# Layer norm of the router inputs in a macaron block: one tile of four on ScalarE, statistics and normalizations interleaved on VectorE

## What is computed

```python
def _layernorm(x, axis=-1, eps=1e-05):
    m = jnp.mean(x, axis=axis, keepdims=True)
    v = jnp.var(x, axis=axis, keepdims=True)
    return (x - m) / jnp.sqrt(v + eps)

x = x + 0.5 * _L0_ffn_ref(_layernorm(x, axis=-1), router_w, wg, wu, wd)
x = x + _L0_attn_ref(_layernorm(x, axis=-1), Wq, bq, Wk, bk, Wv, bv, Wo, bo)
x = x + 0.5 * _L0_ffn_ref(_layernorm(x, axis=-1), router_w, wg, wu, wd)

# in _L0_ffn_ref: router, top two of eight, and the experts
logits = xf @ router_w.T
probs = jax.nn.softmax(logits, axis=-1)
topw, topi = jax.lax.top_k(probs, K)
...
eo = jnp.einsum('ecf,efd->ecd', jax.nn.silu(g) * u, wd)
```

## Time and profile before

| | us |
|---|---|
| median of 3 runs | 1919.36 (1918.79 to 1923.34) |
| profiled execution, its own time | 1917.76 |
| span in the profile | 1916.0 |
| busy PE, PEld | 1616.2, 1275.8 |
| busy DVE, ACT, POOL | 1246.2, 887.6, 874.8 |

### The profile page before, as it was taken

How to read it: one execution, slowest core, us unless ns; L and a number is a source line. 1 busy time by engine, 2 the same in 40 slices (tenths; PEclk the granted TensorE clock), 3 DMA queues, 4 the chain that set the end, 5 groups by cost and what they waited for, 6 DMA issues and landing times.

```text
span 1916.0 us, 40317 instructions
## 1 busy us (share of the span) xinstructions
PE 1616.2 (84%) x13943; PEld 1275.8 (67%) x13943; DVE 1246.2 (65%) x2883; ACT 887.6 (46%) x1627; POOL 874.8 (46%) x636
## 2 busy tenths in 40 slices
PE   4512899999999999995899751289999999999998
PEld 3411687877878787773577641168787787878876
DVE  8987748576574856526898897763745546465551
ACT  4511445445454444535665551144544545445452
POOL 5623262644536354235776652326264452635423
PEclk9999999999999999996999755589999999999999
DMA  6650461614425152226766450045161442515212
GB/s 214 212 185 14 108 122 30 145 41 107 78 70 126 37 132 52 31 29 165 154 146 146 137 195 4 14 108 116 36 145 44 104 83 65 128 42 126 58 25 28
DMA packets 261236, 182.16 MB, mean 95 GB/s; under 512 B 160938, under 2 KB 247860, under 8 KB 261172
## 3 DMA queue, kind: packets, MB, share of 16 engines
q1 hardware_dynamic: 230452, 139.37, 26.7%
q0 software_dynamic: 30720, 41.96, 13.2%
HBM read 89.01 MB, written 54.53 MB: 75 GB/s over the span
## 4 chain that ended last, share of the span: by engine, by line
PE 72%; DVE 12%; issue 6%; POOL 5%; DMA 2%; ACT 2%; DVEq 0%; SPq 0%; POOLq 0%; ACTq 0%
PE bank L1439 43%; PE bank L1452 22%; PE bank L1420 3%; POOL rstd L418 1%; POOL rows L422 1%; DVE kT L1020 1%; DVE rT L1020 1%; PE bank L1400 1%; DVE gat L1229 1%; PE bank L1484 1%; ACT xn L778 1%; DMA xs<-in_L_attn_x 1%; POOL gat L395 1%; DVE xn L937 1%; DVE v L1223 1%
## 5 line engine op out<-in xcount | busy, mean ns | idle before, releaser
L1439 PE MATMUL bank<-xT,w_g 128*128 128x320 f16 x3072 | 503.1, 300 | 30.9 <-DMA xT<-gat 30.9
L1095 DVE SCALAR_TENSOR_TENSOR unit_buf<-bank,sc_cur,unit_buf 128x320 f32<-128x320 f32 x512 | 281.5, 550 | 353.9 <-PE bank L1439 227.9
L1439 PE MATMUL bank<-xT,w_u 128*128 128x320 f16 x3072 | 502.5, 300 | 0.0
L720 ACT ACTIVATE unit_buf<-bank,sc_cur 128x320 f32<-128x320 f32 x512 | 269.5, 526 | 407.1 <-PE bank L1439 405.6
L1452 PE MATMUL bank<-w_d,xs 128*128 128x256 f16 x3840 | 423.8, 273 | 0.0
L1452 PEld LDWEIGHTS bank<-w_d,xs 128*128 128x128 f16 x3840 | 375.2, 98 | 44.4
L1439 PEld LDWEIGHTS bank<-xT,w_g 128*128 128x128 f16 x3072 | 295.7, 99 | 141.0 <-issue 30.6
L389 POOL TENSOR_TENSOR hot_v<-hot_b,val 128x400 bf16<-128x400 bf16 x128 | 147.7, 1154 | 519.9 <-DVE hot_b L1078 519.9
L1439 PEld LDWEIGHTS bank<-xT,w_u 128*128 128x128 f16 x3072 | 301.3, 98 | 117.7
L1101 DVE TENSOR_TENSOR xs<-unit_buf,xs 128x320 f16<-128x320 f32 x512 | 268.0, 523 | 2.2
L395 POOL DMA_INDIRECT gat<-rows_d,id_next x160 | 177.0, 1106 | 200.4 <-DVE id_next L1088 140.0
(11 more groups left out here) (229 smaller groups left out, 1815.2 us busy)
## 6 DMA issues: line engine op xcount, KB each, us to landing
rows_d<-rows SPq DMA_DIRECT2D x32, 512.0 KB, 3.4
raw_gu<-in_L_ffn_wg SPq DMA_DIRECT2D x16, 1024.0 KB, 6.3
raw_gu<-in_L_ffn_wu SPq DMA_DIRECT2D x16, 1024.0 KB, 9.3
raw_d<-in_L_ffn_wd SPq DMA_DIRECT2D x16, 1024.0 KB, 5.5
x_d<-xs SPq DMA_DIRECT2D x1, 8192.0 KB, 32.6
out_x<-xs SPq DMA_DIRECT2D x16, 512.0 KB, 3.7
xs<-in_L_attn_x SPq DMA_DIRECT2D x7, 1024.0 KB, 5.6
xs<-x_d SPq DMA_DIRECT2D x5, 1024.0 KB, 6.1
```

Source lines behind the costliest of these rows:

```text
L720: act.activation(act_s[:, u % 2, :], bank[u % 2][:, 0:CW], ACT.Silu, scale=sc_cur[:, 3:4]).then_inc(S.s_ready, 1)
L1095: dve.scalar_tensor_tensor(h32[:, u % HB, :], bank[2 + u % 2][:, 0:CW], sc_cur[:, 4:5], act_s[:, u % 2, :], mult, mult).then_inc(S.h32_rea ...
L1439: mm = pe.matmul(bank[2 * m + u % 2][:, 0:CW], wgu[m][:, w, k, f * P:(f + 1) * P], xT[:, a * KD + k, c * CW:(c + 1) * CW], start=(j == 0 a ...
```

## The change

ScalarE normalizes the last tile of each group of four (`ACT_TILE`, L671 of the changed kernel), as x times `rstd` plus `nmean`, where `nmean` is minus the mean times `rstd`: VectorE takes minus the mean out of `mv` (one new operation), GpSimd multiplies it with `rstd` behind `power` (one new operation). A semaphore `s_xact` counts ScalarE's tiles; ScalarE waits for it before `high`, and VectorE waits for it before it overwrites `nmean`. VectorE has three `norm` left in a group. A new function `turn(i, r)` issues them between the parts of the next group's statistics: four `bn_stats`, `norm` 0, four `bn_aggr`, `norm` 1, `nmean` and the variance, `norm` 2. The calls of `beside` come two at a time behind each `turn`; before, one stood behind each `stats` and each `norm`. In the second stage ScalarE also waits for `at.lo` before its first tile.

```diff
--- before.py
+++ after.py
@@ -190,6 +190,7 @@
         s_bootx = sem("boot_scale_steps")
         s_passed = sem("waits_passed")
         s_atw = sem("attention_loaded")
+        s_xact = sem("norm_by_act_ready")
 
         def ffn_sems(p):
             names = ("loaded kept stat_ready rstd_ready xn_ready hi_ready lo_ready stored0 stored1 turned turned_ok cent_ready "
@@ -336,6 +337,7 @@
             b, j = q
             return 16 * (QUADS // 2 * b + j // 2 + 1)
 
+        ACT_TILE = G4 - 1
         xt2_flat = xt2[:, :, :, :, :].rearrange("p h t c n -> p h (t c n)")
         FIRST = STEPS - 2
         TURN_BANK = (0, 3)
@@ -416,6 +418,8 @@
                 def power(q, r):
                     pool.wait_ge(S.stat_ready, q + 1)
                     pool.tensor_tensor(rstd[:, r, :], rstd[:, r, :], mhalf[:, :], ALU.pow).then_inc(S.rstd_ready, 1)
+                    pool.wait_ge(S.rstd_ready, 2 * q + 1)
+                    pool.tensor_tensor(nmean[:, r, 0:1], nmean[:, r, 0:1], rstd[:, r, ACT_TILE:], mult).then_inc(S.rstd_ready, 1)
 
                 def low(q, r):
                     pool.wait_ge(S.hi_ready, q + 1)
@@ -662,6 +666,11 @@
 
             def ffn_in(S, head, beside):
                 def high(i, r):
+                    act.wait_ge(S.rstd_ready, 4 * i + 2 * r + 2)
+                    act.wait_ge(S.lo_ready, 2 * i + r + 1)
+                    act.activation(xn[:, r, ACT_TILE, :], tiles(xs, i * PAIR + r * G4 + ACT_TILE, 1)[:, 0], ACT.Identity,
+                                   scale=rstd[:, r, ACT_TILE:], bias=nmean[:, r, 0:1]).then_inc(s_xact, 1)
+                    act.wait_ge(s_xact, 2 * i + r + 1 + (2 * STEPS if S.scaled else 0))
                     act.wait_ge((S.stored0, S.stored1)[r], 16 * i + 16)
                     act.wait_ge(S.xn_ready, 2 * i + r + 1)
                     act.activation(rows[:, r, :, 0:D], xn[:, r, :, :], ACT.Copy).then_inc(S.hi_ready, 1)
@@ -759,6 +768,7 @@
                 else:
                     act.wait_ge(at.gt, B * QUADS - 2)
                     act.wait_ge(at.q, 2 * B * QUADS)
+                    act.wait_ge(at.lo, B * QUADS)
                 ffn_in(S, head, beside)
                 act.wait_ge(S.scales_ready, 1)
                 for loaded in (S.raw_g, S.raw_u):
@@ -922,33 +932,48 @@
                     wait_x(i, r)
                     for g in range(G4):
                         ch.mark(dve.bn_stats(bst[:, r, g, :], tiles(xs, t + g, 1)[:, 0]))
+
+                def moments(r):
                     ch.wait()
                     settle(dve)
                     for g in range(G4):
                         ch.mark(dve.bn_aggr(mv[:, r, g, :], bst[:, r, g, :]))
+
+                def variance(i, r):
                     ch.wait()
+                    settle(dve)
+                    wait_for(dve, s_xact, 2 * i + r - 1 + (2 * STEPS if S.scaled else 0))
+                    dve.tensor_scalar(nmean[:, r, 0:1], mv[:, r, ACT_TILE, 0:1], -1.0, None, mult)
                     dve.tensor_scalar(rstd[:, r, :], mv[:, r, :, 1], EPS, XSCALE ** -2, add, mult).then_inc(S.stat_ready, 1)
 
-                def norm(i, r):
-                    t, q = i * PAIR + r * G4, 2 * i + r
-                    dve.wait_ge(S.lo_ready, q + 1)
-                    dve.wait_ge(S.rstd_ready, q + 1)
-                    for g in range(G4):
-                        last = dve.tensor_scalar(xn[:, r, g, :], tiles(xs, t + g, 1)[:, 0], mv[:, r, g, 0:1],
-                                                 rstd[:, r, g:g + 1], sub, mult)
-                    last.then_inc(S.xn_ready, 1)
+                def norm(i, r, tile):
+                    q = 2 * i + r
+                    if tile == 0:
+                        dve.wait_ge(S.lo_ready, q + 1)
+                        dve.wait_ge(S.rstd_ready, 2 * q + 1)
+                    ins = dve.tensor_scalar(xn[:, r, tile, :], tiles(xs, i * PAIR + r * G4 + tile, 1)[:, 0],
+                                            mv[:, r, tile, 0:1], rstd[:, r, tile:tile + 1], sub, mult)
+                    if tile == ACT_TILE - 1:
+                        ins.then_inc(S.xn_ready, 1)
+
+                def turn(i, r):
+                    n = r ^ 1
+                    stats(i + r, n)
+                    norm(i, r, 0)
+                    moments(n)
+                    norm(i, r, 1)
+                    variance(i + r, n)
+                    norm(i, r, 2)
 
                 def step(i, beside):
-                    stats(i, 1)
-                    beside(4 * i + 1)
-                    norm(i, 0)
-                    beside(4 * i + 2)
-                    stats(i + 1, 0)
-                    beside(4 * i + 3)
-                    norm(i, 1)
-                    beside(4 * i + 4)
+                    for r in range(2):
+                        turn(i, r)
+                        beside(4 * i + 2 * r + 1)
+                        beside(4 * i + 2 * r + 2)
 
                 stats(0, 0)
+                moments(0)
+                variance(0, 0)
                 beside(0)
                 for i in range(head):
                     step(i, beside)
@@ -956,9 +981,9 @@
                     ch.enter(i - head, 2 * 2 * G4)
                     step(i, nothing)
                     ch.leave(STEPS - 1 - head)
-                stats(STEPS - 1, 1)
-                norm(STEPS - 1, 0)
-                norm(STEPS - 1, 1)
+                turn(STEPS - 1, 0)
+                for tile in range(ACT_TILE):
+                    norm(STEPS - 1, 1, tile)
 
             def route(S, ch):
```

## The result

| | us |
|---|---|
| the changed kernel, median of 14 runs | 1924.34 (1923.02 to 1926.28) |
| the kernel before, same chip, median of 14 runs | 1920.03 (1918.02 to 1923.34) |
| ratio, 95% interval | 1.0022 (1.0014 to 1.0030) |
| profiled execution, its own time, and span | 1924.2, 1922.5 |

Slower by 4.3 us, which is inside the 0.3% that the prediction called no change. The interval lies clear of 1, so on this chip the change did cost time, though less than half of the 9.5 us forecast.

The account below looks back on a forecast made before the run. The prediction took the input stages to be bound by a ring of `norm`, `high` and `low`. First stage +3.8 and second +5.65 made +9.5 us on the profiled 1917.76, so 1927.3, and 1929 for the median; range 1921 to 1935.

Parts of the forecast that it names:

- The ring: Input stages' loop: last `norm`, ScalarE's `high`, GpSimd's `low`, then the next group's `norm` held until `low` ends; 4.42 to 4.70 us.
- 0.28 more per group: Steady loop of the input stages: each group of four tiles takes 0.28 us longer, bounds 0 and 0.40.
- GpSimd's 0.03: Steady loop: GpSimd's power and new multiply delay the start of `low` by 0.03 us more on average.
- N: The end of a group's last `norm` on VectorE; `low` was to be allowed by `high` at N + 1.17.
- -0.6 + 3.6 + 0.8: First input stage: group 0 to 1 saves 0.6 us, 13 groups add 3.6, the end at L977 adds 0.8.
- forecast 5.65: Second input stage: 2.8 up to group 8, 0.65 at group 9, 1.4 for five groups, 0.8 at the end.
- The moved product: Second stage: attention's last matrix product (L1234) now stands behind group 2's `norm`, plus 2.2 us; group 4's `high` 2.5 later.
- Groups 5 to 8 add 0.3: Second stage: these groups, bound by the ring or the store of rows, add 0.3 us.
- The `norm` slips in before `low`: Rival, loop: next group's first `norm` goes before `low`; 0.09 more per group, +5.9 us, 1925.3; chance 0.19.
- The power holds VectorE: Rival: the third `norm`, issued beside the power, waits some 1.0 us in each of 28 groups; 1957; chance 0.05.
- The stage absorbs it: Rival: second stage's moved calls cost nothing, ring 0 to 0.1 longer; +1 to +4 us, 1922; chance 0.13.
- Faster: Rival: VectorE's own work is the ring, first `norm` not held by `low`; -0.25 over 28 groups, 1912; chance 0.09.

Follow-up runs that it names:

- low_three_tiles: The kernel before, with GpSimd's `low` over three of a group's four tiles, the fourth's low part not computed: 1908.6 us in one run, against 1920.5.
- the two parts apart: Two kernels, each half the change: ScalarE's tile with VectorE's old order, 2008.2 us; interleaving with four `norm` on VectorE, 2019.3 us; kernel before 2014.4.
- the other two profiles: The changed kernel, unaltered, timed and profiled again on two other chips: 1922.2 us against 1920.5 before, and 2015.9 us against 2014.8.
- after_again: The changed kernel, unaltered, on the chip of the second set: 1922.2 us against 1920.5 for the kernel before, ratio 1.0010.

## Why the prediction was right or wrong

- **The ring, and that the change makes it longer: right.** Shown by low_three_tiles (a shorter `low` gives all of its time back) and by the two parts apart. It holds where the first `norm` stands behind `low`, from the fifth group on.
- **Its price, "0.28 more per group": the step that failed.** It was 0.16. The forecast had 1.38 us behind `low`; it was 1.20. Of the 0.18, 0.10 was the start of the third `norm`, which I took from the gap between variance and `norm` in the loop before; there it is the first `norm` of a group, with waits on two semaphores ahead of it; the third has none of its own and started 0.07 behind the variance (40.81 and 40.88). The rest is in the distances of the starts (0.29, 0.30, 0.07, 0.07, where I had 0.31, 0.33, 0.08, 0.08). GpSimd's 0.03 measured 0.05 here and 0.08 in the other half (N to `low` 1.22 and 1.25). Over 13 and 5 groups 0.12 less takes off some 2.2 us of the forecast.
- **First stage, forecast -0.6 + 3.6 + 0.8.** `low` of group 1 came 0.62 earlier, as forecast. The 13 groups to the fifteenth added 1.9 and not 3.6. "13 groups at one price" was itself wrong: ten of them (from the fifth on) added 1.5, the three ahead of them, with a wait for a store and two starts of `low` at 4.46 and 3.96, added 0.4, and in the other two profiles about 0.1 each. The end of L977 added 0.6. Sum +1.9, which is what the weights show, and not +3.8.
- **Second stage, forecast 5.65.** The moved product held TensorE as said: `high` of group 4 came 2.0 later (forecast 2.5; 0.9 and 1.7 in the other two profiles). "Groups 5 to 8 add 0.3" is the second step that failed, as large as the first: they took 1.9 off in two profiles of three, where the wait of group 8 for a store had shrunk (from 4.62 to 1.14 in the first). From group 8 to end 2 it was +2.5 (forecast 2.85) in these, and +1.2 in the third. Sum +2.6, +1.5 and +2.6; up to the weights +2.3, +1.2 and +2.3.
- **The sum.** The weights give 1.9 + 2.3 = 4.2 in the first pair (the ends 4.9), and the medians lie 4.3 apart. The two profiled executions differ by 6.4; of the other 2.2, 1.6 came in the attention and 0.5 in the first stage's experts, in code that the change doesn't touch, and nothing behind the second stage's weights.
- **The rivals.** *The `norm` slips in before `low`*: not in the steady loop, there by 0.01 in every second group. But it did in some groups of each stage, where `low` came late for another reason; the distances were then 4.46 and 3.96 (3.64 in after_again), not the 4.51 of the rival's sum, since more than one operation got ahead. Its 1925.3 is the nearest of all numbers named, by luck: its ring of 4.51 is not the loop's. *The power holds VectorE*: no. A third `norm` over 1 us, the prediction's sign for it, did occur in after_again (2.04 at 25.27), but it stood behind a late `low` (24.86) and not behind a power. In every row here a `norm` issued behind `low` ends 0.15 behind it (it takes 1.25, 2.13 or 0.89 by when it started), and a `norm` issued inside a power keeps its 0.40. The Trainium skill ("SBUF — State Buffer", "SBUF: two separate sides") says that a GpSimd instruction that starts first has the shared ports for its whole length. The rows agree for `low`, and not for the power. *The stage absorbs it* named 1922 and was nearer than the forecast too: half of it did happen, between groups 4 and 8. *Faster* fell with low_three_tiles.
- **The range** held the result, in its lower third.
